# A two-layer graph network on one core: product P as three one-pass products, centring on ScalarE, graph 0's loads in another order

## The reference, cut to what matters

```
H   = (adj != 0)
Dn  = 1 / (H @ adj[0]);   Be = 1 / H.sum(0)
# first layer, hypergraph convolution twice
h   = relu(Dn * (H @ (Be * (H.T @ (x @ W1.T)))) + b1)
h   = layernorm(h) * gamma + beta
y   = Dn * (H @ (Be * (H.T @ (h @ W2.T)))) + b2 + x
x1  = layernorm(x + y)
# second layer
agg = (adj @ x1) / max(adj.sum(1), 1e-6)
out = layernorm(x1 + relu(concat(x1, agg) @ W.T))
```

## Time and profile before

| | us |
|---|---|
| median of 3 runs | 1109.18 (1108.98 to 1109.61) |
| the profiled execution | 1109.14 |
| its span, first to last instruction | 1107.1 |
| PE busy | 1092.4 (99%) |
| VectorE busy | 700.4 (63%) |
| ScalarE busy | 314.9 (28%) |
| GpSimd busy | 181.2 (16%) |
| granted TensorE clock, mean | 0.999 |

### The profile page before, as it was taken

One profiled execution on the slowest core, in us unless ns is written; L12 is line 12 of the kernel. 1 busy time (PEld: TensorE's weight loads), 2 busy tenths in 40 slices (PEclk: granted clock), 3 DMA queues, 4 the chain that ended last, 5 costly groups with the idle time before them and its releaser, 6 DMA issues.

```text
span 1107.1 us, 18548 instructions
## 1 busy us (share of the span) xinstructions
PE 1092.4 (99%) x6112; PEld 897.1 (81%) x6112; DVE 700.4 (63%) x1846; ACT 314.9 (28%) x705; POOL 181.2 (16%) x256
## 2 busy tenths in 40 slices
PE   7999999999999999999999999999999999999997
PEld 6879697796978969688796887969789697886966
DVE  4665595665955768548685486754766647856326
ACT  4342212422124221333113331143311433024230
POOL 0222004120031102211031110401104020041000
PEclk9999999999999999999999999999999999999999
DMA  7017612066211572124611445115442074300001
GB/s 280 20 39 153 152 41 56 1 151 152 56 39 34 118 152 57 38 65 102 146 47 38 93 104 121 42 38 125 105 93 66 10 152 110 70 9 1 1 1 39
DMA packets 64663, 86.18 MB, mean 78 GB/s; under 512 B 9088, under 2 KB 54784, under 8 KB 64640
## 3 DMA queue, kind: packets, MB, share of 16 engines
q1 hardware_dynamic: 63392, 85.75, 33.7%
q10 hardware_dynamic: 1248, 0.14, 0.1%
HBM read 77.47 MB, written 8.39 MB: 78 GB/s over the span
## 4 chain that ended last, share of the span: by engine, by line
PE 95%; DVE 4%; DMA 1%; ACT 0%; issue 0%; ACTq 0%; DVEq 0%
PE bank L747 40%; PE bank L818 10%; PE bank L856 10%; PE bank L878 10%; PE bank L840 10%; PE bank L775 10%; PE bank L848 3%; PE bank L864 1%; DVE adjT L555 1%; DMA small<-in_L_gnn_gamma_dram 1%; DVE HT L560 1%; PE bank L784 1%; DVE o_f L692 0%; DVE xres L696 0%; ACT m_hi L397 0%
## 5 line engine op out<-in xcount | busy, mean ns | idle before, releaser
L747 PE MATMUL bank<-yv,adjT 128*128 128x257 f32 x1024 | 223.3, 379 | 0.0
L747 PEld LDWEIGHTS bank<-yv,adjT 128*128 128x128 f32 x1024 | 193.6, 189 | 31.8 <-issue 3.8
L402 ACT ACTIVATE small<-mv,small 128x1 f32<-128x1 f32 x192 | 56.6, 295 | 362.5 <-DVE mv L537 266.8
L775 PE MATMUL bank<-x_hi,H 128*128 128x258 f32 x512 | 122.1, 287 | 0.8 <-DVE m_lo L542 0.8
L747 PE MATMUL bank<-x_hi,H 128*128 128x256 f32 x512 | 122.6, 283 | 0.0
L747 PE MATMUL bank<-m_hi,HT 128*128 128x256 f32 x512 | 121.6, 280 | 0.0
L747 PE MATMUL bank<-x_lo,H 128*128 128x256 f32 x512 | 121.1, 280 | 0.0
L747 PE MATMUL bank<-m_lo,HT 128*128 128x256 f32 x512 | 120.9, 279 | 0.0
L542 DVE SCALAR_TENSOR_TENSOR m_lo<-bank,small,m_hi 128x256 fp32r<-128x256 f32 x128 | 61.1, 483 | 94.2 <-ACT m_hi L397 94.1
L840 PE MATMUL bank<-W1T,zT 128*128 128x512 f32 x256 | 120.3, 592 | 0.0
L856 PE MATMUL bank<-gW2T,xnT 128*128 128x256 f32 x512 | 119.8, 379 | 0.0
(11 more groups left out here) (80 smaller groups left out, 1619.4 us busy)
## 6 DMA issues: line engine op xcount, KB each, us to landing
raw<-in_adj_dram SPq DMA_DIRECT2D x112, 256.0 KB, 8.5
adjB<-in_adj_dram SPq DMA_DIRECT2D x224, 128.0 KB, 3.4
x_in<-in_x_dram SPq DMA_DIRECT2D x28, 256.0 KB, 4.4
out_dram<-xres SPq DMA_DIRECT2D x108, 64.0 KB, 1.6
raw<-in_adj_dram SPq DMA_DIRECT2D x4, 1024.0 KB, 13.0
w_row<-in_adj_dram SPq DMA_DIRECT2D x8, 512.0 KB, 3.7
x_in<-in_x_dram SPq DMA_DIRECT2D x1, 1024.0 KB, 7.3
out_dram<-xres SPq DMA_DIRECT2D x4, 256.0 KB, 2.2
```

The source lines that it names most:

```text
L402: nc.scalar.activation(std[:, i:i + 1], mv[:, which, i, 1:2], ACT.Sqrt, bias=eps_c)\
L747: last = mm(bank(stage, i)[:, 0:n_cols], lhsT, rhs, start=(k == 0 and part == 0), stop=(k == NT - 1 and part == parts - 1))
L775: last = mm(*args, start=(c == 0 and n == 0), stop=(c == NT - 1 and n == 1))
```

## The change

- P is made of parts. ScalarE rounds z to `z_high` (scale ROUND_DOWN, fp32r), VectorE subtracts to `z_low`, and `z_cross` = z_high - 4096 z_low. The same is done once with W1. Bank P collects z_high W1_high + z_low W1_low, and a new product M collects z_cross W1_cross. VectorE combines them: first `hrow` = M * rDn_cross + b1, then `hrow` = P * rDn_main + `hrow`. For the first chunk VectorE makes `z_cross`; for the second ScalarE scales and GpSimd subtracts.
- Centring of `hrow` goes to ScalarE (Identity with scale and bias); VectorE makes the bias `shift_h`, one value a row.
- The steps: LAG_T 3 becomes 2, LAG_Q 4 becomes 3, `hrow` has 3 slots and `xnT` 1. Q stands ahead of TH in a step. `SECOND_CHUNK` puts 5 steps k into s = 0 and 3 into s = 1. Q of the last tile moves into S3, behind its step 1, and S3 starts with a group of 4 tiles instead of 2. The bank table is new.
- Set-up of graph 0: adj by single tiles, x in pairs of tiles, in the order of use, weights in between; the weight transposes are put between the matmuls of S1's steps, gamma is applied by ScalarE, and bW2 is summed by VectorE.

```diff
-SECOND_CHUNK = {0: (0, 1, 2), 1: (3, 4), 2: (5, 6), 3: (7,)}
-LAG_T = 3
-LAG_Q = 4
-H_SLOTS = 4
+SECOND_CHUNK = {0: (0, 1, 2, 3, 4), 1: (5, 6, 7)}
+LAG_T = 2
+LAG_Q = 3
+H_SLOTS = 3
...
@@ SyncE, set-up
-            sp.dma_start(W2n[:, :, :], W2.rearrange("(t p) d -> p t d", p=P)).then_inc(W2_loaded, 16)
-            sp.dma_start(x_in[:, :, :], x[0, :, :].rearrange("(t p) d -> p t d", p=P)).then_inc(x_loaded, 16)
             load_first_rows(0)
-            sp.dma_start(W1n[:, :, :], W1.rearrange("(t p) d -> p t d", p=P)).then_inc(W1_loaded, 16)
-            sp.dma_start(WLn[:, :, :], WL.rearrange("(t p) d -> p t d", p=P)).then_inc(WL_loaded, 16)
+            load_first_x(1)
             load_first_rows(1)
             load_first_rows(2)
             load_w(0)
+            load_first_x(2)
             load_first_rows(3)
+            sp.dma_start(W1n[:, :, :], W1.rearrange("(t p) d -> p t d", p=P)).then_inc(W1_loaded, 16)
+            load_first_rows(4)
+            load_first_x(3)
+            load_first_rows(5)
...
@@ GpSimd, each graph
+                for d in range(ND):
+                    pool.wait_ge(z_low_scaled, b * ND + d + 1)
+                    nc.gpsimd.tensor_tensor(z_cross[:, d, CH:2 * CH], z_high[:, d, CH:2 * CH].bitcast(F32),
+                                            z_cross[:, d, CH:2 * CH].bitcast(F32), ALU.subtract).then_inc(z_cross_done, 1)
@@ ScalarE, each graph
+                take_z_high(0)
                 for s in range(NT + LAG_Q):
+                    if s == max(SECOND_CHUNK):
+                        take_z_high(1)
+                    if 0 <= s - 1 < NT:
+                        i = s - 1
+                        act.wait_ge(shift_done, b * NT + i + 1)
+                        nc.scalar.activation(hrow[:, i % H_SLOTS, :], hrow[:, i % H_SLOTS, :], ACT.Identity,
+                                             scale=rstd_h[:, i:i + 1], bias=shift_h[:, i:i + 1])\
+                          .then_inc(normed["h"], 1)
+                    if s == max(SECOND_CHUNK):
+                        scale_z_low()
                     if s < NT:
                         act.wait_ge(*emptied("P", s, b))
                         nc.scalar.activation(hrow[:, s % H_SLOTS, :], hrow[:, s % H_SLOTS, :], ACT.Relu)\
                           .then_inc(relu_done, 1)
+                    if s > LAG_Q:
+                        take_x_hi(s - LAG_Q - 1)
                     if 0 <= s - LAG_T < NT:
+                        act.wait_ge(*full("TH", s - LAG_T, b))
+                        empties_bank(nc.scalar.activation(xnT[:, :, :].rearrange("p k c -> p (k c)"),
+                                                          bank("TH", s - LAG_T)[:, :], ACT.Copy), "TH", s - LAG_T)
                     if s < NT:
                         root("h", 0, std_h, s, b)
@@ VectorE, each graph
+                take_z_low(0)
...
                 for s in range(NT + LAG_Q):
                     if s < NT:
+                        dve.wait_ge(*full("M", s, b))
+                        empties_bank(nc.vector.scalar_tensor_tensor(
+                            out=hrow[:, s % H_SLOTS, :], in0=bank("M", s)[:, :], scalar=rDn_cross[:, s:s + 1],
+                            in1=b1_row[:, :], op0=ALU.mult, op1=ALU.add), "M", s)
+                    if 0 <= s - 1 < NT:
+                        i = s - 1
+                        inverse_root("h", std_h, rstd_h, i, b)
...
+                    if s == max(SECOND_CHUNK):
+                        take_z_low(1)
+                    if s < NT:
                         dve.wait_ge(*full("P", s, b))
+                        dve.wait_ge(*emptied("M", s, b))
                         empties_bank(nc.vector.scalar_tensor_tensor(
+                            out=hrow[:, s % H_SLOTS, :], in0=bank("P", s)[:, :], scalar=rDn_main[:, s:s + 1],
+                            in1=hrow[:, s % H_SLOTS, :], op0=ALU.mult, op1=ALU.add), "P", s)
+                    if s > LAG_Q:
+                        take_q(s - LAG_Q - 1)
                     if s < NT:
                         dve.wait_ge(relu_done, b * NT + s + 1)
                         moments("h", 0, hrow[:, s % H_SLOTS, :], s, b)
@@ TensorE, each graph
+                for s in range(NT + LAG_T):
                     for k in SECOND_CHUNK.get(s, ()):
                         s2_step(1, k)
                     if s < NT:
+                        pe.wait_ge(*free("M", s, b))
...
                         pe.wait_ge(*free("P", s, b))
                         for d in range(ND):
+                            mm(bank("P", s)[:, :], z_high[:, d, nodes], W1_high[:, d, :], start=(d == 0), stop=False)
+                            last = mm(bank("P", s)[:, :], z_low[:, d, nodes], W1_low[:, d, :],
+                                      start=False, stop=(d == ND - 1))
                         fills_bank(last, "P", s)
+                    i = s - LAG_Q
+                    if 0 <= i < NT - 1:
+                        take_product_Q(i)
                     i = s - LAG_T
...
+                      group=4, behind_k=lambda c: take_product_Q(NT - 1) if c == 1 else None)
```

More of the change, by code:

```diff
@@ L55, in graph_net, with add_set @@
     YP = 2 * D + 1
[L61 to L71, removed]
+    BETWEEN = {1: ("gamma",), 3: ("W1", "W1"), 5: ("WL", "WL"), 6: ("W2", "W2")}
+    N_SIDE = TRANSPOSE_BANKS[0]
+    set_of = {}
+    def add_set(name, part):
+        n = len(set_of)
+        set_of[name, part] = TRANSPOSE_BANKS[n % 2], n // 2
+    for c in range(NT):
+        add_set("adj", (c, 0))
+        if c in BETWEEN:
+            add_set(BETWEEN[c][0], 0)
+        add_set("adj", (c, 1))
+        if len(BETWEEN.get(c, ())) > 1:
+            add_set(BETWEEN[c][1], 1)
+    add_set("bW2", 0)
+    setup_fills = [0] * N_SIDE + [(len(set_of) + 1) // 2, len(set_of) // 2]
+    setup_empties = [1] * N_SIDE + setup_fills[N_SIDE:]
+    IN_B = 16 * NB
     OUT_0, OUT_B = 16 * (NT // 2), 16 * NB * (NT // 2)
@@ L435, in graph, with scale_z_low @@
-                take_zT(0)
-                for s in range(NT + LAG_Q):
+                        nc.scalar.activation(z_high[:, d, ch * CH:(ch + 1) * CH], bank("S2", ch * ND + d)[:, :], ACT.Copy,
+                                             scale=ROUND_DOWN).then_inc(z_high_done, 1)
+                def scale_z_low():
+                    for d in range(ND):
+                        act.wait_ge(*emptied("S2", ND + d, b))
+                        nc.scalar.activation(z_cross[:, d, CH:2 * CH], z_low[:, d, CH:2 * CH].bitcast(F32), ACT.Copy,
+                                             scale=SPLIT).then_inc(z_low_scaled, 1)
@@ new lines, in take_q @@
+                def take_q(i):
+                    dve.wait_ge(*full("Q", i, b))
+                    if i >= 2:
+                        dve.wait_ge(q_split, b * NT + i - 1)
+                    empties_bank(nc.vector.tensor_tensor(q_f32[:, i % 2, :], bank("Q", i)[:, 0:D],
+                                                         bW2_row[:, :], ALU.add), "Q", i)
+                take_z_low(0)
+                for d in range(ND):
+                    dve.wait_ge(*emptied("S2", d, b))
+                    nc.vector.scalar_tensor_tensor(
+                        out=z_cross[:, d, 0:CH], in0=z_low[:, d, 0:CH].bitcast(F32), scalar=-SPLIT,
+                        in1=z_high[:, d, 0:CH].bitcast(F32), op0=ALU.mult, op1=ALU.add).then_inc(z_cross_done, 1)
@@ L753, in tiled @@
                     ready(k)
-                    for i in range(GROUP):
+                    for i in range(group):
                         if k == 0:
@@ L757, in tiled @@
                         one(i, k)
-                for i in range(GROUP, NT):
+                    if behind_k:
+                        behind_k(k)
+                for i in range(group, NT):
                     if i == NT - 1 and before_last:
@@ L805, in _ @@
+                    if e == 5 and len(BETWEEN.get(c, ())) > 1:
+                        transpose_set(BETWEEN[c][1], 1)
+                    s1_step(e, c, 0)
+            transpose_set("bW2", 0)
+            for e in range(N_SIDE, NT):
                 pe.wait_ge(*free("S1", e, 0))
@@ L830, in graph, with take_product_Q @@
                 pe.wait_ge(HT_ready, b * NT + NT)
-                for s in range(NT + LAG_Q):
+                def take_product_Q(i):
+                    pe.wait_ge(*free("Q", i, b))
+                    pe.wait_ge(*emptied("TH", i, b))
+                    for k in range(NH):
+                        last = mm(bank("Q", i)[:, 0:D], xnT[:, k, :], gW2T[:, k, :],
+                                  start=(k == 0), stop=(k == NH - 1))
+                    fills_bank(last, "Q", i)
+                for s in range(NT + LAG_T):
                     for k in SECOND_CHUNK.get(s, ()):
@@ L850, in graph @@
                         fills_bank(last, "TH", i)
-                    i = s - LAG_Q
-                    if 0 <= i < NT:
-                        pe.wait_ge(*free("Q", i, b))
```

(5 more changed lines are left out.)

434 lines of the change are left out of this document (250 added, 184 removed), and 15 rows, old and new, of the table PRODUCT_BANKS.

## The result

| | before | after |
|---|---|---|
| median of the runs | 1109.28 us (1108.98 to 1109.61, 4 runs) | 1141.39 us (1140.52 to 1143.39, 4 runs) |
| profiled execution, its span | 1109.1, 1107.1 | 1140.64, 1139.0 |
| mean granted clock | 1.00 | 0.99 |
| ratio | | 1.0292 (95%: 1.0278 to 1.0306) |

The kernel became 2.9% slower. The forecast was 1127 with a range of 1116 to 1146: the sign and the stalls held, the size came out 14 us short. The narrower own range, 1121 to 1134, was missed. The wide range holds only because it took in the rival of the lower clock, whose 1144 lies nearer to the measured time than the forecast does.

What follows compares the result with a forecast made beforehand. PE was taken as the bound, busy 1092.4 of 1107.1 us. From 1109.1, set-up gave -6 and eight graphs +24 (shorter P -2.6, stalls +5.6 a graph), making 1127 us; range 1116 to 1146, own range 1121 to 1134.

Steps and rivals of the forecast that it cites:

- the sign: Whole kernel: the change makes it slower, chance 0.84, against faster 0.12 and same 0.04.
- The narrower own range: Whole kernel: 1121 to 1134 us around the forecast of 1127, inside the wider range of 1116 to 1146.
- the rival of the lower clock: Stall ahead of each graph's first Q: idle PE drops to half clock, 17 us more in all, 1144; chance 0.14.
- The path of a tile: P stage, steady part: VectorE's new loop takes 3.31 us a tile against PE's 3.56, so PE stays the bound.
- The twin: VectorE in the P stage: the unseen M operation costs the same as the P operation, 0.66 us start to start.
- P by PE: P stage: two fp32 matmuls of 1.72 us a tile become six one-pass ones of 1.40, gaining 20.8 us in all.
- The three stalls: P stage, each graph: PE waits 3.66 us ahead of Q0 and 0.98 each ahead of Q5 and Q6, +5.6 together.
- The two late ones: End of the P stage: with one xnT buffer, TH's drain, copy and restart cost 0.98 us before Q5 and Q6 each.
- the z_low of 1.24 us: Start of the P stage: VectorE's two take_z_low(1) operations stand ahead of P1's operation and delay it, ending at 11.74.
- the three tiles in a row: Start of the P stage: three P tiles go by in 4.6 us while VectorE needs 3.31 for each.
- the sum: Whole kernel: 1109.1 less 6 for set-up plus 24 for eight graphs gives 1127 us; clock loss kept out as a rival.
- Set-up: Graph 0: S1 begins near 6.1 instead of 12.34, S2 near 33; 6 us less in all (4 to 8).

Runs made afterwards that it cites:

- e1: Changed kernel with ScalarE copying the first TH bank to xnT one step earlier, in step 1 ahead of tile 2's ReLU: 1136.36 us (1.0247).
- e3: Changed kernel with two xnT buffers and TH ahead of Q in a step of PE: 1122.19 us (1.0126).
- e4: Changed kernel with P as three products in one bank, low x low, M and z_cross left out: 1123.36 us (1.0126).
- e5: e4 with S2's second chunk spread 3/2/3, z_low of that chunk behind P's operation, TH ahead of Q, two xnT buffers: 1089.21 us (0.9821).
- e2: Changed kernel with twelve unread matmuls on PE ahead of the first Q of each graph, waits kept: 1130.88 us (1.0194).
- e6: Kernel before with only the new set-up of graph 0, its P stage kept: 1106.83 us (0.9979).
- e7: e5 with VectorE's bW2 sums and row sums of tiles 4 to 7, and GpSimd's residual, put later in set-up: 1087.78 us (0.9809).
- e8: Changed kernel with centring of hrow moved back from ScalarE to VectorE: 1149.8 us (1.0372).

## Why the prediction was right, and where its size was off

**The path of a tile: right.** Forecast 3.31 us a tile on VectorE; measured 3.26 and 3.30 in graph 2. The twin (M's operation, 0.63 where 0.66 was taken) and the shift (0.13 start to start) held; z_low was 0.59 a piece from start to start where 0.62 was taken. ScalarE's centring is 0.81 long, between the bounds of 0.63 and 0.95, and costs next to nothing: ReLU starts 0.84 behind the start on P's bank where 0.79 was taken.

**P by PE: right.** 1.39 for six matmuls against 1.40, 0.23 each in M and P as in S2.

**The three stalls: right.** PE's stream stopped at 337.3 and Q0 began at 340.59, with 1.99 instead of 1.73 for its eight at full clock: 3.3 + 0.26 = 3.6 where 3.66 was forecast. The two late ones are 0.75 and 0.65 plus 0.25 each, so 1.0 and 0.9 against 0.98. Net per graph 2.95 against 3.0. e1, e3 and e4 each took away the piece that the forecast's order names and got a smaller stall, never none; e5 took all and got 0.2 us of waiting for xnT in the whole run. Not shown apart are the two pieces that the forecast put at the start of the stage, the z_low of 1.24 us and the three tiles in a row: only e5 changed them, both at once.

**The clock: mis-weighed.** The rival "the idle PE falls to the lower clock" stood at 0.14 as a case apart, 17 us dearer. It was true in six graphs of eight, at 1.7 us (2.1 was worked out), in all 10.2 us where the sum had nothing; e2 shows it by itself with 9.6 to 10.5. That the measured time still lies in the stated range is owed to the 0.14 given to this rival, not to the sum. The Trainium skill, TensorE: Matmul & The Clock Gate, Part 1, says that an idle PE is throttled again; this trace agrees, with a granted clock of 0.63 behind the stall. What failed was the argument against it: that no row of before shows a fall was no evidence, because no steady stretch of before has PE idle.

**Set-up: mis-sized.** The term "I take 6 us less (4 to 8)" measured about 2 in after and 2.3 in e6. Its first half was right: S1 began early. Timeline of PE in set-up, which answers to the earlier trace rows:

```profile
6.01 0.55 PE L900 MATMUL bank<-x_hi,H 128*128 128x258 f32 x1 [0.54 <-issue]
...
29.31 0.39 PE L900 MATMUL bank<-x_lo,H 128*128 128x256 f32 x1 [0.89 <-DVE H L598]
...
34.83 0.39 PE L900 MATMUL bank<-x_hi,H 128*128 128x258 f32 x1 [1.24 <-DVE bW_row L721]
...
36.85 0.40 PE L960 MATMUL bank<-HT,m_hi 128*128 128x512 f32 x1
```

S1 begins at 6.01 where 6.1 was forecast and 12.34 was before, but S2 only at 36.85 against 39.17. In S2 PE waited once more, 0.4 us at 43.00, for an m_lo behind row sums. The sum looked at PE and the loads alone. The engines in the stretches of the end (columns: PE, its weight loads, VectorE, ScalarE, GpSimd, clock, DMA share, GB/s):

```profile
24.00:32.00 8.00, 6.49 (x53) 5.93 (x52) 7.76 (x21) 4.71 (x11) 0.04 (x1) 1.00 0.02 8
32.00:43.10 11.10, 9.48 (x55) 7.85 (x53) 10.89 (x29) 3.99 (x9) 11.10 (x12) 1.00 0.01 1
```

VectorE is busy for 97% and 98% of them. The trace of before already had it full in the first stretch, while PE was full too:

```profile
24.00:32.00 8.00, 8.00 (x73) 8.00 (x72) 8.00 (x14) 3.54 (x7) 0.00 (x0) 1.00 0.00 0
```

In after, once the last adj tile had landed it had H, x_lo, HT, row sums and the sums for bW2 to make, in one queue, and PE waited for it. That this order held it up is shown by e7, which gains up to 1.9 us by it. An estimate for S2, forecast near 33 and begun at 36.85: PE's waits for VectorE between 24 us and S2 are 0.6, 0.89 and 1.24, together 2.7 where the sum had none; and S1's matmuls start 0.21 us apart until about 10.2 and 0.12 later, so some 2 us were lost to the slow clock there, about 0.6 more than the sum allowed. That is 3.3 of the 3.8 us; what is left was not followed.

**The sum, mended by measurement.** 1109.1 - 2.0 + 8 × 2.95 + 6 × 1.7 = 1140.9, against 1140.64. The 2.0 is what the difference leaves, so the agreement proves nothing by itself; the other two terms are read from the marks. Against the forecast of 1127, the clock is the larger miss (10.2) and set-up the other (4).

## What to carry to other kernels

A cheaper operation on the engine that bounds a stage pays only if every other engine's loop is shorter than the new step with room to spare, and the start of the stage has to be laid out order by order: here a margin of 0.25 us a tile could not take up 1.24 us of z_low and three tiles that came in 4.6 us, though what each of these two did was not measured apart. Price an idle stretch of a few us on PE at its length and at up to 1.7 us more for the clock behind it, even when the trace before shows no fall, as it may have nothing to show it with. And count an early start as gained only up to the next queue that is full: a start 6.3 us earlier was worth 2.3 at S2, and up to 1.9 more lay in the order of VectorE's and GpSimd's work.

## What the runs showed of the hardware that was not expected

- PE's clock fell after idle stretches of 2.17 us (e4, one graph of eight), 2.25 us (e3, four of eight) and 2.36 us (e1, four of eight), after 3.54 us in all eight (e8; granted clock 0.55 from 342.40 to 346.00), and in e4's set-up after two short ones of 1.33 and 0.49, yet not after 3.2 us in two graphs of after. The length of the idle stretch alone does not decide; what else does stays open.
- Work that nobody reads can shorten a kernel: 96 more matmuls, and 10.5 us less between the medians (e2).
- ScalarE's scale and shift by row (Identity, 128x512) took 0.81 us where its ReLU of the same tile took 0.62. GpSimd took 1.28 us for a subtraction of 512 columns.
- VectorE's row sum of 1024 columns took 1.22 us at 29.77 and 1.53 to 1.59 at 36.70 to 41.00, where GpSimd was busy all the time (11.10 of 11.10 us). In e7, where GpSimd starts only behind them, the same sums take 1.22 to 1.23, as in this line:

```profile
38.13 1.23 DVE L588 SCALAR_TENSOR_TENSOR unread<-raw,w_row 128x1024 bf16<-128x1024 f32 x1
```

  GpSimd is slower too: its first eight residual operations take 6.57 us in e5, beside VectorE's sums, and 4.62 in e7, behind them. It is not so for every operation: in e5 the sum at 35.84 takes 1.24 though GpSimd is under way from 33.10. Which accesses of the two collide was not tried.
